# Seven half-size products instead of eight for the output projection and the feed-forward base, and later stages run one after the other

## What is computed

```
y  = x @ W_cond.T + 0.5 * (x @ A[label].T) @ Bc.T         # rank 32, A chosen by sequence
q, k, v = split(y @ w_qkv.T + b_qkv)                      # 32 heads of 32, 8 key/value heads
attn = softmax(causal(rope(q) @ rope(k).T / sqrt(32))) @ v
x1 = x + attn @ w_o.T + b_o
h  = x1 @ W2.T + 2 * mixture(x1; Wr, A2, B2, language)    # 8 experts of rank 16, 2 picked
f  = h @ W_base.T + b_base + 2 * mixture(h; W_router, A, B)
out = x1 + f
```

## Time and profile before

| what | value |
|---|---|
| median of 3 runs | 1208.04 us (1207.91 to 1208.53) |
| profiled execution | 1208.27 us, its span 1206.5 us |
| PE busy | 1185.5 us (98%) |
| DVE, ACT, POOL busy | 54%, 31%, 26% |
| DMA moved | 74.53 MB, mean 62 GB/s |

### The profile page before, as it was taken

How to read it: one execution, slowest core, us unless ns; L and a number is a source line. 1 busy time by engine, 2 the same in 40 slices (tenths; PEclk the granted TensorE clock), 3 DMA queues, 4 the chain that set the end, 5 groups by cost and what they waited for, 6 DMA issues and landing times.

```text
span 1206.5 us, 20242 instructions
## 1 busy us (share of the span) xinstructions
PE 1185.5 (98%) x7376; PEld 1061.4 (88%) x7376; DVE 648.2 (54%) x1234; ACT 368.3 (31%) x1125; POOL 313.0 (26%) x186
## 2 busy tenths in 40 slices
...
GB/s 248 36 36 52 9 113 85 51 54 43 52 43 43 43 43 57 48 43 30 118 45 88 109 71 141 60 63 52 52 52 52 52 52 52 52 52 52 52 35 35
DMA packets 30307, 74.53 MB, mean 62 GB/s; under 512 B 4290, under 2 KB 8898, under 8 KB 30274
## 3 DMA queue, kind: packets, MB, share of 16 engines
...
## 4 chain that ended last, share of the span: by engine, by line
PE 93%; DVE 4%; DMA 1%; ACT 1%; issue 1%; SPq 0%; POOL 0%; DVEq 0%; ACTq 0%
PE psum L1003 22%; PE psum L370 20%; PE psum L1556 19%; PE psum L1514 14%; PE psum L1065 4%; PE psum L1035 4%; PE psum L1531 2%; PE psum L1050 2%; PE psum L1539 2%; PE psum L1022 1%; PE psum L1082 1%; PE psum L1547 1%; DVE low L873 1%; DMA w_raw<-in_w_cond 1%; DVE w_l L1339 0%
## 5 line engine op out<-in xcount | busy, mean ns | idle before, releaser
L370 PE MATMUL psum<-c_high_low,w_h 128*128 128x256 f32 (+1 forms) x1344 | 238.6, 288 | 7.1 <-ACT w_h L480 5.4
L1556 PE MATMUL psum<-fr_h,c_high_low 128*128 128x512 f32 (+1 forms) x768 | 213.0, 361 | 0.1
L370 PEld LDWEIGHTS psum<-c_high_low,w_h 128*128 128x128 f32 x1344 | 205.0, 193 | 7.7 <-issue 5.4
L1003 PE MATMUL psum<-p_h,c_high_low 128*128 128x512 f32 (+1 forms) x768 | 196.4, 359 | 0.5 <-DVE qkv L960 0.5
L370 PE MATMUL psum<-c_high_low,w_l 128*128 128x256 f32 (+1 forms) x704 | 177.3, 278 | 0.0
L1514 PE MATMUL psum<-w_h,c_high_low 128*128 128x512 f32 x512 | 170.3, 397 | 0.6 <-DVE w_l L1339 0.6
L1556 PEld LDWEIGHTS psum<-fr_h,c_high_low 128*128 128x128 f32 x768 | 136.5, 188 | 22.6 <-issue 0.3
L1003 PEld LDWEIGHTS psum<-p_h,c_high_low 128*128 128x128 f32 x768 | 133.5, 188 | 13.3 <-issue 0.7
L1556 PE MATMUL psum<-fr_l,c_high_low 128*128 128x512 f32 (+1 forms) x384 | 138.3, 360 | 0.0
L1397 POOL TENSOR_TENSOR x_out<-x,spare 128x1024 f32<-128x1024 f32 x16 | 38.8, 2422 | 349.3 <-DMA out<-x_out 330.6
L370 PEld LDWEIGHTS psum<-c_high_low,w_l 128*128 128x128 f32 x704 | 127.3, 192 | 0.0
...
## 6 DMA issues: line engine op xcount, KB each, us to landing
...
attn_scratch<-ring SPq DMA_DIRECT2D x16, 512.0 KB, 2.6
...
ring<-in_x_tok SPq DMA_DIRECT2D x16, 512.0 KB, 3.3
out<-x_out SPq DMA_DIRECT2D x15, 512.0 KB, 3.2
ring<-in_wqkv_t SPq DMA_DIRECT2D x11, 512.0 KB, 4.7
ring<-in_last_t SPq DMA_DIRECT2D x10, 512.0 KB, 4.7
...
```

The source lines that it names most:

```text
L370: mm = pe.matmul(to, stationary, moving, start=start and n == 0, stop=k == KT - 1 and n == len(passes) - 1, skip_group_check=True)
L1003: mm = pe.matmul(to, sx[:, k, :], moving(w, n, k), start=first, stop=False, skip_group_check=True)
L1556: mm = pe.matmul(b_ps[:, n, 0:cols.stop - cols.start], s[:, k, :], w[:, k, cols], start=first, stop=n == 2 and k == KT - 1 and s is x1t_l)
```

## The change

**Products.** Two units (256 tokens) are taken as one. For output projection and feed-forward base the 256 x 1024 input and the 1024 x 1024 matrix are cut in half both ways, and the four 128 x 512 outputs come from seven half-size products (12 matmuls of 512 columns each) in Winograd's form instead of eight. This needs sums of input blocks (s1 to s4, made by POOL from the raw values, then split like all others), sums of weight blocks (t1 to t4), copies of products out of PSUM (e1, e5, e6, e7, by ACT), and adds of these copies to the residual (by DVE).

**Stages.** Output projection becomes a stage of its own (`projection`), between attention and `folding_ffn`: x1 and its transpose go to DRAM buffers and are read back by the feed-forward. Products p1, p2, p5, p6, p3 of the first pair stand in the attention drain in the place of the fold's matmuls, and the weights of the projection (b11, b21, b22, t1 to t4; 2048 columns each) are made there and in two attention steps. `folding_ffn` uses three chunks of 392, 384 and 384 columns and starts after the projection. POOL's two rotation sums in attention go to DVE (`combine`).

The diff, cut to its core (`wo` is the projection, `ff` the feed-forward, both of class `Winograd`; p counts pairs):

```diff
 # Winograd
+    BLOCK = {"p1": "a11", "p2": "a12", "p3": "s4", "p4": "a22", "p5": "s1", "p6": "s2", "p7": "s3"}
+    WEIGHT = {"p1": "b11", "p2": "b21", "p3": "b22", "p4": "t4", "p5": "t1", "p6": "t2", "p7": "t3"}
+    BANK_OF = {"p1": "a", "p2": "a", "p6": "b", "p7": "b", "p4": "b", "p5": "c", "p3": "c"}
...
+    def sums(self, pool, p, name):
+        for u in range(BPU):
+            pool.wait_ge(self.raw_in[u], 16 * self.times(p + 1))
+        self.free(pool, p, name)          # the product of this block, one pair back, is done
+        one, two, how, count = {"s1": (self.part("a21"), self.part("a22"), ALU.add, 0),
+                                "s2": (self.source("s1"), self.part("a11"), ALU.subtract, 1),
+                                "s4": (self.part("a12"), self.source("s2"), ALU.subtract, 2),
+                                "s3": (self.part("a11"), self.part("a21"), ALU.subtract, 3)}[name]
+        need(pool, self.summed, 4 * self.times(p) + count)
+        pool.tensor_tensor(self.source(name), one, two, how).then_inc(self.summed, 1)
...
+    def low(self, engine, p, name):
+        engine.wait_ge(self.block_high[name], self.times(p + 1, name))
+        if name in ("s1", "s2"):          # the sum that still reads this block's raw values
+            engine.wait_ge(self.summed, 4 * self.times(p) + {"s1": 2, "s2": 3}[name])
...
+    def product(self, pe, p, name):
+        pe.wait_ge(self.block_low[block], self.times(p + 1))
+        for before in {"p1": ("c11",), "p5": ("c12",), "p6": ("c21",)}.get(name, ()):
+            need(pe, self.out[before], self.times(p))
+        for copy in {"p2": ("e1",), "p3": ("e5",), "p7": ("e6",), "p4": ("e7",)}.get(name, ()):
+            pe.wait_ge(self.copied, self.copied_at(p, copy))
+        for k in range(HALF):
+            for n, (s, w) in enumerate(((bh, wh), (bh, wl), (bl, wh))):
+                mm = pe.matmul(self.banks[self.BANK_OF[name]], s[:, k, :], w[:, k, :, :], ...)
 # attention, last units: w = 14, v = 15
+        def drain():                      # scalar
+            probs_high(w, 0); values_high(v); wo.high(act, 0, "a12"); wo.copy(act, 0, "e1")
+            values_out(w, 0); probs_high(w, 1); wo.high_weight(act, "t1"); values_out(w, 1)
+            keys_queries(v); values_apart(v)
+            wo.high_weight(act, "b22"); wo.high_weight(act, "t2"); wo.high(act, 0, "s2"); wo.copy(act, 0, "e5")
+            exp_scores(v, 0, False)
+            wo.high(act, 0, "s4"); wo.high(act, 0, "a22"); wo.high(act, 0, "s3"); wo.copy(act, 0, "e6")
+            probs_high(v, 0); exp_scores(v, 1, False); values_out(v, 0)
+            wo.high_weight(act, "t3"); probs_high(v, 1); wo.high_weight(act, "t4"); values_out(v, 1)
+        def drain():                      # gpsimd
+            wo.low_weight(pool, "b21"); wo.weight_sum(pool, "t1")
+            wo.sums(pool, 0, "s2"); wo.sums(pool, 0, "s4")
+            wo.weight_sum(pool, "t2"); wo.weight_sum(pool, "t3"); wo.sums(pool, 0, "s3")
+            normalise(v, 0); wo.weight_sum(pool, "t4"); normalise(v, 1)
+        def drain():                      # vector
+            wo.low(dve, 0, "a12"); probs_low(w, 0); rotate_both(v); values_low(v); probs_low(w, 1)
+            keys_queries(v); wo.low_weight(dve, "t1"); wo.low(dve, 0, "s1")
+            last_queries(v); values_apart(v); less_max(v, 0)
+            wo.low_weight(dve, "t2"); wo.low(dve, 0, "s2"); sum_up(v, 0); inverse(v, 0); less_max(v, 1)
+            wo.low(dve, 0, "s4"); wo.low_weight(dve, "b22"); probs_low(v, 0); sum_up(v, 1); inverse(v, 1)
+            wo.low(dve, 0, "a22"); wo.low(dve, 0, "s3"); wo.low_weight(dve, "t3"); probs_low(v, 1); wo.low_weight(dve, "t4")
+        def drain():                      # tensor
+            transpose_p(w, 0); pe.wait_ge(qkv_out, UNITS); wo.product(pe, 0, "p1")
+            attend(w, 0); transpose_p(w, 1); wo.product(pe, 0, "p2")
+            attend(w, 1); transpose_qk(v, (0, 1)); transpose_qk(v, (2,)); wo.product(pe, 0, "p5")
+            scores(v, 0); scores(v, 1); wo.product(pe, 0, "p6")
+            transpose_p(v, 0); wo.product(pe, 0, "p3"); attend(v, 0); transpose_p(v, 1); attend(v, 1)
 # attention, unit 1
+            if score and not value:
+                wo.high_weight(act, "b11")          # scalar, after values_apart
+                wo.low_weight(dve, "b11")           # vector, ahead of less_max(v, 0)
 # projection, step p of pairs 1 to 6
+    sync:   wait lows a11, a12, s3, a22 of p; load_raw(p + 1); store_turned(p - 1, 0 and 1);
+            store(p, 0); load_tokens(p + 1, 0); store(p, 1); load_tokens(p + 1, 1)
+    scalar: copy e1(p), turned(p - 1, 0), high a11(p + 1), copy e5(p), high s1(p + 1), copy e6(p),
+            turned(p - 1, 1), high s2, a12(p + 1), copy e7(p), high s4, s3, a22(p + 1)
+    gpsimd: bias(p, 0), bias(p, 1), sums s1, s2, s4, s3 (p + 1)
+    vector: low a11(p + 1), add 0 to 2(p), low s1(p + 1), add 3, low s2(p + 1), add 4, move c11(p),
+            low a12(p + 1), move c22, c12(p), low s4, s3, a22(p + 1), move c21(p)
+    tensor: p1, turn(p - 1, 0), p5, p6, turn(p - 1, 1), p2, p7, p3, p4
 # feed_forward, step p
+    tensor: gates(p, 0), gates(p, 1), p1, p5, turn_z 0, p6, up_gates, p2, p7, turn_z 1, p3,
+            up_base c11, c12, p4, up_base c21, c22
+    vector: route(p, 0), low_z 0, add 0 to 2, low a11, a21 (p + 1), add 3, low s1, route(p, 1), low_z 1,
+            add 4, low s2, a12, add 5, low s4, s3, finished c11, c12, low a22, finished c21, c22
+    sync:   wait lows a11, a12, s1, s3, a22 of p; load_raw(p + 1); store both units, load their residuals
```

1814 lines of the change are left out of this document (1211 added, 603 removed).

## The result

The changed kernel takes **1320.3 us** (median of 4 runs, 1318.0 to 1323.5); the kernel before, on the same chip, 1208.3 us. The ratio is 1.0925 (95% interval 1.0912 to 1.0938): slower by 9%. The direction was forecast, the size was not: 1255 was the forecast and 1270 the upper end of its range.

The account below looks back on a forecast made before the run. The prediction took the kernel as bound by TensorE (PE), busy 98%. Its terms, from 592.9 us for attention through drain, projection, fold and feed-forward, summed to 1253.6; plus 1.5 gave 1255 us, range 1202 to 1270 (forecast's own 1225 to 1270).

Parts of the forecast that it names:

- the drain: End of attention: the last unit's softmax shares its time with making the Strassen weights; 76 us (bounds 58, 80).
- Rival A: Attention's end and c11: DVE hardly waits for POOL, so the kernel becomes faster, 1205 us; chance 0.14.
- the lock: DVE operations with two SBUF inputs and POOL operations exclude each other for a whole instruction and take turns.
- The 55 us of work on the pair: Attention's end: 31 us of POOL and 24 us of DVE work need the shared pair and cannot overlap.
- Unit 1: Attention loop: DVE splits a weight block that ACT must first round, so L928 slips by 2.9 us (bounds 1, 3).
- The removed matmuls and the fold: Output projection and base product save 43.8 us of matmuls; folding saves 7 and takes 115 with transposes.
- the step that failed is 4: Projection pairs 1 to 6: 20.9 us of PE work plus two waits, 24.3 per pair (22.5, 25.5), 146 altogether.
- wait (b): Projection pairs: ACT's copy e6 stands behind rounding that needs the next pair's load, so p7 waits 0.4 to 2.7 us.
- e6: Projection pairs: ACT's copy of a product, for which p7 waits; forecast to follow at 17.5 to 19.8 us after p3.
- Rival C: Transfers bind: 4 MB per projection pair in bursts, waits feeding each other; 27 us per pair, 1275 total; chance 0.15.
- the step that failed is 7: Feed-forward pairs 1 to 7: 32.4 us each without idle PE, s2 chain covered; 227 us (226, 230).
- Pair 7 and the first feed-forward pair: Last projection pair to folding's start: 29 us (25.5, 31); first feed-forward pair, up_gates late: 54 us (45, 56).

Follow-up runs that it names:

- best2: Changed kernel with reordered work in projection, feed-forward, drain and unit 1, also ACT's and DVE's in pair 7 and ACT's in the first feed-forward pair: 1242.3 us.
- pj_copies: Changed kernel with two of ACT's product copies and the second turned half moved ahead of rounding the next pair's blocks in the projection: 1291.6 us.
- pj_c11: Changed kernel with DVE's c11 sum in the projection moved ahead of a low part and an add that had stood before it: 1317.1 us.
- ff_route2: Changed kernel with POOL's feed-forward bias after the first routing, and DVE's second routing and second z_low ahead of most adds and lows: 1296.2 us.

## Why the prediction was right or wrong

**The direction, and the drain.** The direction was right. The drain was put at 76 us and took 79, and the walk through the written order, from which that figure comes, held: it had the scores end at 628.4 with the last qkv sum at 590.0, and they ended at 635.9 with that sum at 595.6, so 1.9 us later; the second max subtraction came 1.7 us late, the end of p4 7 us with the 4 us for half-clock starts not yet counted. Rival A (the lock costs little, drain 55, 1205) fell: even with 25 us of that work left out the drain took 61. The 55 us of work on the pair are a weaker reason than the walk, since the pair was free for 20 us of the 79; DVE's and POOL's operations count there as links of a chain too.

**Unit 1: mis-sized.** L928's counterpart ended its wait 3.1 us later, as costed (2.9). The term stopped at DVE: the exponentials and the low of the ranks follow it, PE's hole grew from 1.8 to 4.6 us, and behind it four products took 1.48 us instead of 0.97. That made 4.2 us in unit 1; 1.4 more came over the other units, the upper end of the 0 to 1.5 given for DVE's two rotation sums.

**The removed matmuls and the fold.** Right: 552 instructions fewer, the fold 116.6 for 115, and where hardly anything waits a pair of the feed-forward takes 32.5 (best2) for 32.4. The 43.8 us of the seven products for eight are there. It is smaller than what the change adds around it.

**Projection pairs: the step that failed is 4.** The forecast of 24.3 us was 20.9 of work and 3.4 for two waits, with nothing for the half clock. The measured 28.2 are 21.1 of work (a pair of pj_copies with a fast p1, less its hole), 2.0 and 2.6 us for the two waits, and 2.5 us more, nearly all of it products at the lower clock: five of six p7 took 4.4 to 4.6 us instead of 3.0, three of six p1 4.2 to 4.9. So the largest part of the miss is the half-clock piece behind each hole, which I had priced for the drain and put at nothing in the loop.

The second part is wait (b). In the pair at 767 the rounding of s1, behind which e6 stands, came late because the second half of the raw tile did:

```profile
778.57 0.63 ACT L1303 ACTIVATE ring<-ring_plain 128x512 fp32r<-128x512 f32 x1 [6.64 <-DMA ring_plain<-attn_scratch]
...
780.35 1.43 POOL L1294 TENSOR_TENSOR c_high_low_plain<-ring_plain 128x512 f32<-128x512 f32 x1 [0.84 <-DMA ring_plain<-attn_scratch]
```

p3 had ended at 762.4, so this half landed 18.0 us behind it, where 15 to 17.3 had been given; sum, rounding and copy then took 2.6 us, costed at 2.5. The waits were also treated as independent. pj_c11 shows that they are not: c11 taken out of the way gave 3 us in all, not 12. Rival C had the waits feed each other and 27 us per pair; the measured 28.2 lies beyond it. It was C's mechanism in ACT's order: with ACT's copies ahead of the roundings, the same transfers allowed 22.4 us.

**Feed-forward pairs: the step that failed is 7.** "Without idle PE" was wrong: 2.9 us of holes a pair on the mean and 0.8 us of slower products behind them, the largest miss. I checked there the one chain that I knew from the projection (s2) and found it covered. I did not lay POOL's bias beside DVE's routing, although the lock and its rule stood in the prediction, and although the diff gives both orders: POOL begins the bias when the residual lands, DVE its routing when the gates are done, and both fall at the same point of each pair. Thirteen steps of 0.17 to 0.4 us looked too small to matter. A step under the lock costs the POOL operation it waits for (1.26 us), whatever its own length. ff_route2 shows it: the same work in another order, 32.7.

**Pair 7 and the first feed-forward pair.** Both waits were named with their cause (ACT's weight rows; z_low behind lows and behind ACT's rounding of a11) and came out 5 and 4 us longer. best2 shows that the wait for the second turn was all order, ACT's and DVE's together (both were moved), and the wait for `up_gates` one third.

**The range.** Its upper end added up the parts' upper ends only as far as 1280 and was cut to 1270. The parts for both loops had upper ends of 25.5 and 32.9 per pair, 153 and 230 us, where 169 and 253 were measured. A stage that runs six or seven times needs the wider bound, since a hole of 3 us there is worth as much as the whole uncertainty of the drain.
